# Selective-scan block: shared FFN computed transposed, its residual added on TensorE, LN3's rstd on ScalarE, and the first and last steps in another order

## The reference

```python
h = h + mamba(layernorm(h))      # xz = x @ W_in; causal conv of 4 taps; silu; B, C, dt from xc;
                                 # delta = softplus(dt @ W_dt + b_dt); 16 states per channel:
                                 # s = exp(delta*A)*s + delta*B*xc;  y = sum(C*s) + D*xc
                                 # out = (y * silu(z)) @ W_out
h = h + ffn(layernorm(h))
```

## Time and profile before

| | |
|---|---|
| median of 3 runs | 1827.78 us (1824.47 to 1832.68) |
| the profiled execution | 1829.5 us |
| its span in the trace | 1827.4 us |
| instructions | 28123 |
| busy: GpSimd, VectorE, TensorE, ScalarE | 1635.6, 1598.0, 1540.8, 1294.5 us |
| steady steps | 51.4 us each, in the middle of the run |

### The profile page before, as it was taken

The page is one execution under the profiler, slowest core; times in us unless marked ns, Lnnn a source line. Parts: engine busy times, 40 slices in busy tenths (PEclk is TensorE's granted clock), DMA queues, the critical chain, the costliest instruction groups (busy, mean ns, idle before and its releaser), DMA issues.

```text
span 1827.4 us, 28123 instructions
## 1 busy us (share of the span) xinstructions
PE 1540.8 (84%) x9760; PEld 1065.7 (58%) x9760; DVE 1598.0 (87%) x1579; ACT 1294.5 (71%) x3038; POOL 1635.6 (90%) x909
## 2 busy tenths in 40 slices
PE   7678888888898888888898888888988888887688
PEld 6555656565666555655665556656655566654345
DVE  2589999999889999999889999998899999888935
ACT  2567777777767777777777777777777777766534
POOL 0699999999999999999999999999999999999715
PEclk8898999999889999999989999999899999886679
DMA  4855564545555645455566444555564545455110
GB/s 122 198 117 138 133 141 116 121 119 118 116 132 138 142 117 120 118 121 126 119 138 143 118 117 121 121 125 119 138 143 120 121 115 119 116 115 134 34 27 20
DMA packets 173471, 218.12 MB, mean 119 GB/s; under 512 B 68955, under 2 KB 163813, under 8 KB 172818
## 3 DMA queue, kind: packets, MB, share of 16 engines
q1 hardware_dynamic: 172754, 215.17, 50.2%
q0 software_dynamic: 576, 1.17, 0.3%
HBM read 170.05 MB, written 46.62 MB: 119 GB/s over the span
## 4 chain that ended last, share of the span: by engine, by line
POOL 70%; issue 14%; PE 7%; DVE 5%; ACT 2%; DMA 2%; SPq 0%; POOLq 0%; DVEq 0%; ACTq 0%
POOL xr L1437 46%; POOL xr L1445 18%; POOL u L1453 3%; POOL ob L1460 2%; DVE psum L1102 2%; DVE xr L1102 2%; PE psum L530 1%; POOL rs L1468 1%; PE psum L648 1%; PE psum L673 1%; PE psum L821 1%; ACT psum L870 1%; PE psum L785 1%; PE psum L541 0%; PE psum L674 0%
## 5 line engine op out<-in xcount | busy, mean ns | idle before, releaser
L1437 POOL TENSOR_TENSOR xr<-u,bbc 128x912 f32<-128x912 f32 x512 | 1076.9, 2129 | 11.7 <-DMA u<-u_scratch 11.7
L870 ACT ACTIVATE psum<-delta,a_neg 128x228 f32<-128x228 f32 x2048 | 801.1, 439 | 310.1 <-DVE xr L1111 236.0
L1102 DVE TENSOR_TENSOR_SCAN psum<-psum,xr 128x912 f32<-128x912 f32 x320 | 656.8, 2052 | 94.0 <-ACT psum L870 86.4
L1445 POOL TENSOR_TENSOR xr<-xr,cbc 128x912 f32<-128x912 f32 x192 | 407.9, 2125 | 69.7 <-DVE xr L1102 69.7
L1102 DVE TENSOR_TENSOR_SCAN xr<-psum,xr 128x912 f32<-128x912 f32 x192 | 392.2, 2043 | 3.2 <-ACT psum L870 3.2
L631 PE MATMUL psum<-xr,fold 128*32 128x228 f32 x4096 | 325.7, 415 | 61.4 <-POOL xr L1445 50.8
L1111 DVE TENSOR_TENSOR xr<-psum,cbc 128x912 f32<-128x912 f32 x320 | 353.7, 1105 | 11.4 <-DVE psum L1102 0.5
L530 PE MATMUL psum<-xh,win 128*128 128x228 f32 x1024 | 220.3, 370 | 13.4 <-ACT xs L901 8.8
L631 PEld LDWEIGHTS psum<-xr,fold 128*32 128x32 f32 x4096 | 100.1, 118 | 225.5 <-issue 119.2
L576 PE MATMUL psum<-xi,conv_d 128*128 128x228 f32 x1024 | 224.1, 373 | 0.0
L530 PEld LDWEIGHTS psum<-xh,win 128*128 128x128 f32 x1024 | 198.3, 197 | 32.8 <-issue 14.0
(11 more groups left out here) (174 smaller groups left out, 1607.1 us busy)
## 6 DMA issues: line engine op xcount, KB each, us to landing
u<-u_scratch SPq DMA_DIRECT2D x256, 228.0 KB, 4.2
delta<-delta_scratch SPq DMA_DIRECT2D x256, 228.0 KB, 6.6
bbc<-bc_scratch SPq DMA_DIRECT2D x128, 114.0 KB, 2.5
cbc<-bc_scratch SPq DMA_DIRECT2D x128, 114.0 KB, 2.7
u_scratch<-u SPq DMA_DIRECT2D x64, 228.0 KB, 2.4
delta_scratch<-delta SPq DMA_DIRECT2D x64, 226.0 KB, 6.1
h_scratch<-h SPq DMA_DIRECT2D x32, 228.0 KB
out<-ob SPq DMA_DIRECT2D x32, 228.0 KB
```

Of the source, the lines that this page charges most:

```text
L870: ins = nc.scalar.activation(slot(k)[:, j * TOK:(j + 1) * TOK], delta4[:, c // 2, j, c % 2], ACT.Exp, scale=a_neg[:, c, j, n:n + 1])
L1102: nc.vector.tensor_tensor_scan(x if k in ON_POOL else slot(k), slot(k), x, 0.0, ALU.mult, ALU.add).then_inc(scan_done, 1)
L1437: nc.gpsimd.tensor_tensor(xr[:, k % XRING], u4[:, c // 2, :, c % 2], bbc[:, p, n].unsqueeze(1).to_broadcast([P, J, TOK]), ALU.mult).then_i ...
L1445: nc.gpsimd.tensor_tensor(xr[:, k % XRING], xr[:, k % XRING], cbc[:, p, k % NI].unsqueeze(1).to_broadcast([P, J, TOK]), ALU.mult).then_inc ...
```

## The change

- The shared FFN is computed with the hidden size in partitions and the tokens in columns: `ffn_in` multiplies by the FFN weights as the stationary side, the biases b1 and b2 become per-partition scalars (ScalarE's `bias`, VectorE's `scalar`), and the bias rows on TensorE are gone, as are `v_turn` and `vt_copy`.
- LN3: `v_center` (TensorE, centring matrix), `v_square` (ScalarE), `v_var` (TensorE, mean matrix), `ln3_rstd` (ScalarE, Ln and Exp, 228 columns, into `gate`), `v_norm` (VectorE, multiplication of v by it, at k = 4). The statistics on VectorE and the power on GpSimd are gone.
- `ffn_out` adds the residual: a matrix `plus` of 115 rows (identity and a row of ones) times h2 with the bias b3 as its 115th row. `out_copy` on ScalarE (k = 6) brings the result to SBUF. `ffn_residual` and `residual_bias` are gone. `h2` has two buffers, `ob` one. `proj_delta` waits for `out_copy` as it waited for `ffn_residual`.
- `tokens` treats two groups in one pass at even steps (144 columns), `image_tokens` follows twice; patches are loaded in pairs; HRING is 5.
- `softplus_abs` and `delta_out` work on all four chunks in one instruction, `u_out` too.
- ON_POOL is 1, 3, 8, 10, 12, 14. Places: `proj_z` k = 13, `convolve(0)` k = 9, `ffn_gate` k = 15, `normalize` k = 9, `y_out(0)` k = 10, `dbl_copy` k = 4, `h2_scale` k = 3, `square` k = 5, x_out k = 12 and 13.
- Step -1 and step 32 have lists of their own (`before_first`, `after_last`), the spread of the first group takes delta ahead of u, and the expert part takes the FFN of the last groups earlier.

```diff
-ON_POOL = (1, 4, 7, 9, 12, 14)
+ON_POOL = (1, 3, 8, 10, 12, 14)
-    XRING, SLOTS, HRING = 8, 2, 4
+    XRING, SLOTS, HRING = 8, 2, 5
...
                     def ffn_in(g):
...
+                        for a in range(2):
                             for k in range(DC):
-                                pe.matmul(f12_ps[:, s], x2t[:, k, s], w12[:, k], start=(k == 0), stop=False)
-                            mm = pe.matmul(f12_ps[:, s], ones[0:1, 0:T], b12[0:1], start=False, stop=True)
+                                mm = pe.matmul(f12_ps(g)[:, a], w12[:, k, a * H:(a + 1) * H], x2t[:, k].rearrange("p s t -> p (s t)"),
+                                               start=(k == 0), stop=(k == DC - 1))
...
+                    def v_center(g):
...
+                        pe.matmul(vc_ps(g), cent_h[:], vv_of(g), start=True, stop=True).then_inc(vc_mm, 1)
+
+                    def v_var(g):
+                        pe.wait_ge(vsq_done, g + 1)
+                        pe.matmul(vvar_ps(g), mean_w[:], vsq[:], start=True, stop=True).then_inc(vvar_mm, 1)
...
+                        pe.wait_ge(vn_done, g + 1)
                         for s in range(SEQ):
-                            mm = pe.matmul(f3_ps[:, s], vt[:, s], w3[:], start=True, stop=True)
+                            pe.matmul(f3_ps(g)[:, s], plus[0:T + 1], h2_of(g)[0:T + 1, s], start=True, stop=False)
+                            mm = pe.matmul(f3_ps(g)[:, s], vv_of(g)[:, s * T:(s + 1) * T], w3[:], start=False, stop=True)
                         mm.then_inc(f3_mm, 1)
...
+                    def before_first():
+                        proj_bcdt(0, 0)
+                        proj_delta(0)
+                        tokens(1, 1)
+                        center(1)
+                        fold_means()
+                        var(1)
+                        for half in range(2):
+                            proj_x(1, 1, half)
+                        for half in range(2):
+                            convolve(1, half)
+                        for half in range(2):
+                            proj_z(0, 0, half)
...
+                            if k == 0 and runs(i - 3):
+                                v_center(i - 3)
+                            if k == 0 and i % 2 == 0 and runs(i + 2):
+                                tokens(i + 2, 2)
                             if k == 1 and runs(i + 1):
                                 proj_bcdt(i + 1, 1 - p)
...
+                            if k == 3 and runs(i - 3):
                                 ffn_out(i - 3)
                             if k == 3 and runs(i + 1):
                                 proj_delta(i + 1)
...
+                            if k == 13 and runs(i + 1):
+                                proj_z(i + 1, 1 - p, 0)
+                            if k == 13 and runs(i + 1):
+                                proj_z(i + 1, 1 - p, 1)
...
+                    def v_square(g):
+                        act.wait_ge(vc_mm, g + 1)
+                        nc.scalar.activation(vsq[:], vc_ps(g), ACT.Square).then_inc(vsq_done, 1)
+
+                    def ln3_rstd(g):
+
+                        act.wait_ge(vvar_mm, g + 1)
+                        nc.scalar.activation(vsq[:], vvar_ps(g), ACT.Ln, bias=eps[:, 0:1], scale=DM / H).then_inc(lv3_done, 1)
+                        act.wait_ge(lv3_done, g + 1)
+                        nc.scalar.activation(gate_of(g), vsq[:], ACT.Exp, scale=-0.5).then_inc(rs3_done, 1)
+
+                    def out_copy(g):
+                        act.wait_ge(f3_mm, g + 1)
+                        need(act, out_out, 16 * g)
+                        nc.scalar.activation(ob[0:T], f3_ps(g), ACT.Copy).then_inc(o_done, 1)
...
+                            if k == 2 and runs(i - 3):
+                                v_square(i - 3)
+                            if k == 5 and runs(i - 3):
+                                ln3_rstd(i - 3)
+                            if k == 6 and runs(i - 3):
+                                out_copy(i - 3)
...
+                    def v_norm(g):
                         dve.wait_ge(rs3_done, g + 1)
...
+                        nc.vector.tensor_tensor(vv_of(g), vv_of(g), gate_of(g), ALU.mult).then_inc(vn_done, 1)
...
-                            if k == 13 and runs(i - 2):
+                            if k == 15 and runs(i - 2):
                                 ffn_gate(i - 2)
...
+                            if k == 4 and runs(i - 3):
+                                v_norm(i - 3)
```

More of the change, by code:

```diff
@@ L249, in fusion_kernel @@
             const_ev = sem("const_ev")
+            bias_in = sem("bias_in")
             gw_in = sem("gw_in")
@@ L383, in runs, with over_steps @@
                 return not isinstance(g, int) or 0 <= g < GROUPS
-            def over_steps(e, body, first=None, ready=None, last=None):
+            def over_steps(e, body, first=None, ready=None, later=None, last=None):
                 for i in range(-2, GROUPS + 1):
@@ L390, in over_steps @@
                     else:
-                        body(i, i % HRING)
+                        body(i)
                     if i == -1 and ready is not None:
                         ready()
+                    if i == 1 and later is not None:
+                        later()
                     if i == GROUPS - 1 and last is not None:
@@ L450, in rows_out, with spread_tensor @@
                                          rows.partition_broadcast(DQ)).then_inc(done, 16)
-                    def body(i, r):
-                        p = (r + 1) % 2
-                        if runs(i + 3):
+                    def spread_tensor(g, half, scratch, dst, stored, count, done):
+                        need(sp, dbu_done, UNITS * (g - 1) + UNITS // 2 * (half + 1))
+                        need(sp, exp_done, UNITS * (g - 1) + UNITS // 2 * (half + 1))
+                        sp.wait_ge(stored[half], count)
+                        spread(scratch, dst, half, done)
@@ L1028, in ready, with last_bias, bias_of_last @@
                         act.wait_ge(const_dve, CONST_DVE)
+                        act.wait_ge(const_ev, 1)
+                    def last_bias():
                         act.wait_ge(const_ev, 3)
-                    over_steps(act, body, first, ready)
+                        for half in range(2):
+                            for s in range(SEQ):
+                                act.dma_start(h2[T:T + 1, half, s], b3[0:1]).then_inc(bias_in, 16)
+                    def bias_of_last():
+                        act.wait_ge(delta_done, 2 * GROUPS)
+                        for s in range(SEQ):
+                            act.dma_start(h2_of(GROUPS - 1)[T:T + 1, s], b3[0:1]).then_inc(bias_in, 16)
+                    over_steps(act, body, first, ready, last_bias, bias_of_last)
                     def expert_rstd(m):
```

556 lines of the change are left out of this document (314 added, 242 removed).

## The result

The changed kernel takes 1780.9 us (median of four), the kernel before 1827.0 on the same chip: a ratio of 0.974 (95% interval 0.971 to 0.976), 2.6% faster, 46 us by the medians. Three of the four runs lie between 1778.6 and 1781.4; the fourth ran in a slower state, 1806.4 us at a granted clock of 0.81 in place of 0.93, and is left out of the ratio. The forecast was 1771, the range 1738 to 1818. The profiled execution took 1780.39 us with a span of 1778.0, against 1829.5 and 1827.4.

The account below looks back on a forecast made before the run. It took a loop through GpSimd's products, reduction, z projection and silu, 51.4 us a step, as the bound. 1829.5 less 44 (steady part), 6 (head) and 8 (tail) gave 1771.5, or 1770 against the median; forecast 1771, range 1738 to 1818.

Parts of the forecast that it names:

- The steady part: Loop over groups: 28 full-FFN steps gain 1.5 us each, the first three 0.7, together 44 us.
- two loops: Kernel before: 51.4 us a step through GpSimd and z; VectorE then ScalarE, 41.7 + 9.7 less what ScalarE would not wait.
- VectorE, unit 2 to unit 15, and ScalarE: VectorE stretch 41.7 to 40.4 us, with 0.35 for the rstd multiplication; ScalarE's stretch 9.7 to 9.1; step 49.5.
- one on the clock: Rule weighed against the forecast: matmul groups separated by waits drop TensorE to the lower clock every round.
- The new chain: Scan 2 through output projection and copy to delta: 0.4 us spare in odd steps, 0.6 to 0.8 paid in even; mean 49.85.
- Rival 2: Low clock moves onto output and delta projections, 3.9 us more against 0.4 spare: steps of 53.0, 1866 us; chance 0.06.
- rival 3: Chain to delta late by 2 us on average, through part-time clock falls or even steps: no steady gain, 1815; chance 0.13.
- The slow pairs: Four pairs of neighbouring steps at 53.3 and 54.9 us, 22 us in all, left as they are.
- The z projection: Moved ahead of the reductions of units 14 and 15: done at 793.8 instead of 794.5, ScalarE's stretch 9.7 to 9.1.
- Head: Before the loop: exponentials start earlier because projections precede tokens and centring; 4 to 9 us, taken as 6.
- Tail: After the loop: gather starts about 9 us earlier, expert stage 5 to 9; gain 3 to 14 us, taken as 8.
- Signs: Right: scans 49.5 and 50.2 apart, z silu wait under 0.5. Wrong: delta projection at half clock, first scan after 61 us.

Follow-up runs that it names:

- 4: Kernel before, GpSimd's residual addition and LN3 operations replaced by 2-element fills (output lacks residual and LN3's rstd): 1837.6 us, ratio 1.006.
- 9: Kernel before, with only the z projection moved from unit 14 to unit 13: 1873.2 us, ratio 1.025.
- 12: Kernel before, GpSimd's residual addition and LN3 operations replaced by fills, and z projection at unit 13: 1874.5 us, ratio 1.027.
- 1: Changed kernel, LN3's rstd written by ScalarE to PSUM instead of the SBUF tile gate: 1744.0 us, ratio 0.953.
- 11: Changed kernel with 12 filler matmuls in odd steps, plus the multiplication by rstd split into two instructions of 114 columns: 1869.4 us, ratio 1.023.
- Experiment 2: Changed kernel, 12 filler matmuls of 144 columns on TensorE in odd steps, where even steps have tokens: 1762.3 us, ratio 0.964.
- 3: Changed kernel, z projection put back from unit 13 to unit 14: 1791.9 us, ratio 0.980.
- 7: Changed kernel, patch loads of groups 2 and 3 issued ahead of group 0's delta and u stores in the head: 1778.1 us, ratio 0.971.
- 5: Kernel before, the eight center matmuls issued three times over, 16 matmuls more ahead of ffn_out: 1945.0 us, ratio 1.064.
- 10: Kernel before, second half of the x projection issued twice, 8 matmuls ahead of the h2 copy wait: 1842.1 us, ratio 1.008.

## Why the prediction was right, and where not

**The total** came out within 10 us, but partly through errors that cancel. The steady part was to give 44 and gave 40.1, the head 6 and 2.1, the tail 8 and 7.2 (1.5 of it before the last product): 58 and 49.4 us. The ordinary step gained 1.19 us and not 1.5; and in the steady part 22 us were won and 20 lost that the prediction had not counted.

**What bounds the kernel before.** Named as two loops, 51.4 through GpSimd and z, and VectorE and ScalarE's, 51.4 less what ScalarE would not wait, at most its 0.99 (50.4). Experiments 4, 9 and 12 agree but for the size: with the first loop shortened by either edit, or by both, the step stops at 50.93. That what stops it is the second loop is argued from this. GpSimd's loop was ahead by 0.44 us a step only, and its 70% of the chain was worth no more.

**VectorE, unit 2 to unit 15, and ScalarE.** Predicted 40.4 and 9.1, measured 41.1 (678.69 to 719.79) and 9.08 in an even step. The error in the first is the term that no row showed: the multiplication by rstd at 0.35 (0.2 to 0.6) measured 1.09 and 1.51. The nearest row, the gate product, has one operand in PSUM; the new one has both in SBUF. Experiments 1 and 11 give the mechanism: it waits until the GpSimd instruction under way has ended. In the changed kernel:

```profile
686.02 6.44 POOL L1629 TENSOR_TENSOR xr<-u,bbc 128x912 f32<-128x912 f32 x3
```

The first of these three products ends at about 688.15, the multiplication started at 687.30 and ends at 688.39; in the odd step the product ends at 738.3 and the multiplication at 738.57. The Trainium skill (SBUF — State Buffer, section "SBUF: two separate sides") has this rule: an instruction of VectorE with two SBUF inputs and one of GpSimd exclude each other for the length of the instruction, and do not share bandwidth. The runs agree (2.18 us for 114 columns), and this was the rule that spoke against the change; the prediction did not weigh it, but one on the clock. With 0.38 the step is 49.48 in even steps, just the 40.4 + 9.1 of the prediction, and 49.05 in odd ones, where VectorE has no image addition either.

**The new chain.** Its 0.6 to 0.8 in even steps did not come: an even step shows no wait before delta. The tokens were to push TensorE's queue back; but TensorE has caught up before the output projection and waits 1.23 us for the multiplication there. In odd steps, where the chain was to have 0.4 us to spare, it was late in 10, by the clock: the output projection took 3.6 us in place of 2.1. Rival 2 named this place; it had both projections at half clock and a step 3.5 us late (3.9 less the 0.4), where the delta projection keeps its 1.77 us, the waits are 0.8 to 2.9, and 11 steps of 31 are hit. A clock that falls in a third of the steps stood only in a part of rival 3. Experiment 2 shows that it is the clock.

**The slow pairs** were left as they are, 22 us, without a cause. They vanished, and 20.0 us of other long steps took their place: two sums that have nothing to do with each other. In the changed kernel TensorE runs from the h2 projection to the convolution without that wait of 1.42 (700.57 to 719.99), at a granted clock of 1.00 from 708.7 on; and over the 7.5 us that begin 0.5 us into the FFN's first projection it is 1.00 in every full step. That the missing wait is what made the pairs vanish is argued, not tried.

**The z projection.** The 0.6 (by the prediction's own times of 794.5 and 793.8 it would be 0.7) was 0.44 in the kernel before (9); in the changed kernel, where GpSimd no longer closes the loop, the move gives 0.08 in ordinary steps (3). ScalarE's 9.1 came out, but in part by luck: the second z silu starts 0.43 earlier in the stretch (5.58 us behind 719.82, before 6.01 behind 788.53), with 0.78 of its wait left where under 0.5 was expected, and the other 0.17 lies behind it, between that silu and scan 2, without a cause that the rows show. The prediction counted two remedies, but each alone suffices.

**GpSimd.** Own work 48.0 to 48.2 (48.0), waits of 0.15 at product 3 and 0.80 at product 8 (0.2 and 0.9), no loop through it: as predicted. One more wait, 1.09 for delta ahead of u, was not named.

**Head.** 6 predicted, 2.1 measured. The exponentials start 7.6 earlier (55.68, before 63.26), within the 4 to 9. The step that failed is taking them for the bound: the first scan waits for GpSimd's product, and that for the u rows, which the new order puts behind the delta rows, so that this product starts 1.0 later than before (60.00, before 59.03). The scan came 2.6 earlier (62.22, before 64.86). Behind it the patch loads, moved behind all of these on SyncE, cost VectorE 5.6 us (7). Patches counted in no line of the prediction's head.

**Tail.** 8 predicted; 5.7 behind the last product by C, and 1.5 in the last step. The gather starts at 1701.54, 14.0 behind the last product of unit 15 (before 20.2), so 6 and not 9 earlier, and the gate logits come behind the FFN of the last group:

```profile
1723.57 0.20 DVE L1544 TENSOR_TENSOR sc<-psum,gb 128x36 f32<-128x36 f32 x1 [6.67 <-PE psum L902]
```

**Signs.** Of those named: the steps were 50.2 in even ones but never 49.5 in odd; the wait of the z silu was 0.78, not under 0.5; GpSimd's waits stood where they should. VectorE's wait before delta was over 0.5 in the 10 long odd steps. Of the signs of being wrong one came true: the first scan was still after 61 us (62.22), and it pointed at the head. "TensorE's delta projection at half clock" was the right thing to look for, one projection too late: it was the output projection.

## What to carry to other kernels

An instruction of VectorE with two SBUF operands, placed beside a busy GpSimd, is to be priced at its own time plus what is left of the GpSimd instruction, each time; one operand in PSUM brought it from 1.09 and 1.51 us back to 0.38, here 37 us of 1781 with the long steps that went with it. The engine with the largest share of the chain may be ahead of the next loop by less than 1%: find the second loop's length before counting what relief of the first is worth, and don't count two edits that remove the same wait twice. Where thinned-out matmuls leave two waits close together, look at the granted clock behind them; some work put there in time kept it in experiment 2, where it stood in a place in which TensorE waits anyway, and cost more than it gave in 5 and 10, where others wait for what stands behind it. The clock of a whole step hides this: take it over the instructions that the chain runs through.

## What the runs showed of the hardware

The clock of TensorE fell to half (0.54) behind two waits of 1.30 and 1.75 us within 4 us, and in four steps behind 1.31 and 0.61 us (1); and behind the same wait of 1.42 us in some steps and not in others of one run (the kernel before, 4 and 9). With twelve matmuls of 144 columns, done 7 us before those waits were over (727.7 and 734.5), it was 1.00 at the output projection in every full step (2). A fall costs only where the chain runs: in ordinary odd steps of the changed kernel the clock of the step is 0.93 as well. VectorE's product of 228 columns took 0.39, 1.09 or 1.51 us by what GpSimd was doing; 114 columns took 0.27 or 2.18.
